# Row maxima of the attention softmax, taken over half of the heads at a time

## What is computed

```python
q = split_heads(x @ wq + bq)                 # h = 8 heads of 48
k = split_heads(x @ wk + bk)
v = split_heads(x @ wv + bv)
scores = jnp.einsum('bhqd,bhkd->bhqk', q, k) * scaling
scores = scores + attn_bias[:, None, :, :]   # attn_bias is the adjacency
attn = jax.nn.softmax(scores, axis=-1)
ctx = jnp.einsum('bhij,bhjd->bhid', attn, v)
...
x = _rmsnorm(x + attn_out, alpha1, gamma1)
ff = jax.nn.silu(x @ w1 + b1) @ w2 + b2
x = _rmsnorm(x + ff, alpha2, gamma2)
```

## Time and profile before

| what | value |
|---|---|
| median of 3 runs | 3242.74 us (3239.6 to 3253.91) |
| the profiled execution, its own time | 3253.83 us |
| span of that execution, first to last instruction | 3252.0 us |
| mean granted TensorE clock in it | 0.969 of full speed |
| TensorE matmul busy, share of the span | 2958.8 us, 91% |
| VectorE busy | 1908.7 us, 59% |
| ScalarE busy | 1540.4 us, 47% |
| GpSimd busy | 1444.2 us, 44% |

### The profile page before, as it was taken

The page is one execution under the profiler, slowest core; times in us unless marked ns, Lnnn a source line. Parts: engine busy times, 40 slices in busy tenths (PEclk is TensorE's granted clock), DMA queues, the critical chain, the costliest instruction groups (busy, mean ns, idle before and its releaser), DMA issues. The chain is left out here.

```text
span 3252.0 us, 63751 instructions
## 1 busy us (share of the span) xinstructions
PE 2958.8 (91%) x21571; PEld 2841.3 (87%) x21571; DVE 1908.7 (59%) x3165; ACT 1540.4 (47%) x3998; POOL 1444.2 (44%) x1406
## 2 busy tenths in 40 slices
PE   3999999999999999999999757788899999999986
PEld 3899999999999999999999747688899999999983
DVE  4456565565656565656555457455676766666754
ACT  3354545455454545454545334355454444454530
POOL 0334344444444343434444447200466766666650
PEclk9999999999999999999999979899999999999998
DMA  4001001010101010100101056455666666666869
GB/s 123 29 23 44 24 31 37 24 44 24 44 24 44 24 44 23 43 24 29 38 24 39 28 230 271 132 169 156 200 210 205 197 190 185 209 192 193 261 225 362
DMA packets 293655, 359.10 MB, mean 110 GB/s; under 512 B 24328, under 2 KB 285960, under 8 KB 293512
## 3 DMA queue, kind: packets, MB, share of 16 engines
q1 hardware_dynamic: 284840, 344.92, 33.0%
q10 hardware_dynamic: 8704, 12.58, 1.0%
HBM read 286.14 MB, written 71.30 MB: 110 GB/s over the span
## 5 line engine op out<-in xcount | busy, mean ns | idle before, releaser
L1611 PE MATMUL u_bank<-x_in,x_w 128*128 128x256 f32 x4608 | 585.4, 286 | 27.9 <-issue 17.4
L1611 PEld LDWEIGHTS u_bank<-x_in,x_w 128*128 128x128 f32 x4608 | 578.8, 195 | 30.3 <-issue 30.3
L929 POOL TENSOR_TENSOR hT_lo<-h_tmp,hT_hi 128x512 fp32r<-128x512 f32 x192 | 247.8, 1291 | 471.0 <-DVE hT_hi L817 471.0
L1764 POOL TENSOR_TENSOR x_w<-raw,x_w 128x768 fp32r<-128x768 f32 x128 | 274.1, 2141 | 296.2 <-DVE x_w L1707 296.2
L1768 POOL TENSOR_TENSOR x_aT<-x_act,x_aT 128x512 fp32r<-128x512 f32 x128 | 299.3, 2338 | 217.2 <-ACT x_aT L1676 217.2
L390 PE MATMUL m_bank<-yT_hi,w_hi 128*128 128x256 f32 x1152 | 339.7, 295 | 0.0
L1667 ACT ACTIVATE x_gelu<-u_bank,x_b1T 128x256 f32<-128x256 f32 x256 | 121.3, 474 | 444.8 <-PE u_bank L1611 444.8
L390 PE MATMUL m_bank<-yT_lo,w_hi 128*128 128x256 f32 x1152 | 324.5, 282 | 0.0
L390 PE MATMUL m_bank<-yT_hi,w_lo 128*128 128x256 f32 x1152 | 323.7, 281 | 0.0
L663 ACT ACTIVATE h_tmp<-m_bank,b1c 128x256 f32<-128x256 f32 x384 | 160.6, 470 | 330.1 <-PE m_bank L390 329.7
L1623 PE MATMUL o_bank<-x_w,x_aT 128*128 128x384 f32 x1536 | 289.6, 336 | 1.8 <-POOL x_aT L1768 1.8
(11 more groups left out here) (213 smaller groups left out, 7343.0 us busy)
## 6 DMA issues: line engine op xcount, KB each, us to landing
raw<-in_L_ffn_w_dram SPq DMA_DIRECT2D x384, 384.0 KB, 5.0
ws_raw<-in_L_ffn_w_slot_dram SPq DMA_DIRECT2D x8, 2304.0 KB, 9.4
x_in<-in_x_dram SPq DMA_DIRECT2D x32, 384.0 KB, 3.5
x_res<-in_x_dram SPq DMA_DIRECT2D x32, 384.0 KB, 4.2
residual<-f_sb SPq DMA_DIRECT2D x32, 384.0 KB, 2.5
yn<-yn_sb SPq DMA_DIRECT2D x32, 384.0 KB, 2.5
yk<-yn SPq DMA_DIRECT2D x16, 768.0 KB, 11.1
se<-se SPq DMA_DIRECT2D x16, 768.0 KB, 3.3
```

The source lines that it names most:

```text
L929: nc.gpsimd.tensor_tensor(hT[i % 3][1][:], h_tmp[i % 2][:], hT[i % 3][0][:].bitcast(F32), ALU.subtract).then_inc(hl.sem, 1)
L1611: mm = pe.matmul(u_bank[n % BANKS][:, g, :], w1s[i % 2][a][:, c, g, c2 * P:(c2 + 1) * P], xT[e % 2][b][:, c, :], start=c == 0 and j == 0, ...
L1764: nc.gpsimd.tensor_tensor(w2s[i % 2][1][:], raw2[i][:], w2s[i % 2][0][:].bitcast(F32), ALU.subtract).then_inc(w2_lo.sem, 1)
```

## The change

Every addition of the adjacency is followed directly by a reduction over the four heads of its half, and there is one signal for each half (four in a step, where there were two). ScalarE waits in front of each group of four exponentials for the maxima of that half. The same elements are reduced, and the values are the same.

```diff
-    sc_ok, mx_ok, p_ok, rs_ok = S("scores", 4), S("row_max", 2), S("exp", 16), S("recip", 2)
+    sc_ok, mx_ok, p_ok, rs_ok = S("scores", 4), S("row_max", 4), S("exp", 16), S("recip", 2)
...
             def exps(g, t):
-                act.wait_ge(mx_ok.sem, mx_ok.at(g, t + 1))
                 for par in range(2):
+                    act.wait_ge(mx_ok.sem, mx_ok.at(g, 2 * t + par + 1))
                     for m in range(H // 2):
...
                                             adj_sb[:, t, :].unsqueeze(1).broadcast_to([P, H // 2, P]), ALU.add).then_inc(sc_ok.sem, 1)
-                dve.wait_ge(sc_ok.sem, sc_ok.at(g, 2 * t + 2))
-                nc.vector.tensor_reduce(nmax[:, t, :], s_sb[t][:].rearrange("p a m n -> p (a m) n"), X_AXIS, ALU.max,
-                                        negate=True).then_inc(mx_ok.sem, 1)
+                    dve.wait_ge(sc_ok.sem, sc_ok.at(g, 2 * t + par + 1))
+                    nc.vector.tensor_reduce(nmax[:, t, par * (H // 2):(par + 1) * (H // 2)], s_sb[t][:, par, :, :], X_AXIS,
+                                            ALU.max, negate=True).then_inc(mx_ok.sem, 1)
```

## The result

| | before | after |
|---|---|---|
| median of the runs made together (4 and 4) | 3244.45 us | 3210.32 us (3205.1 to 3213.1) |
| ratio, after to before | | 0.9889, 95% interval 0.9863 to 0.9916 |
| profiled execution, its own time / span | 3253.83 / 3252.0 us | 3213.1 / 3211.3 us |
| one step of the layer | 55.64 us | 54.52 us |

The change makes the kernel faster by 1.1%, 34 us. The forecast was 36.5 us less and 3206 us, in a range of 3197 to 3230. It started from the 3242.74 of three runs; from the 3244.45 of four the same gain would have given 3208.

The account below looks back on a forecast made before the run. TensorE was taken to bound the kernel, losing time only while transposes wait for the exponentials. Starting these 1.14 us earlier in 32 steps gives 36.5 us: 3242.74 - 36.5 = 3206 us, range 3197 to 3230.

Parts of the forecast that it names:

- What bounds the kernel: Layer's regular steps: TensorE bounds, losing time only where transposes of the exponentials (L449) wait for them, 32.7 of 1600 us.
- The price of a half: VectorE's maxima over 512 elements: r = 0.69 us, on a line between 0.42 for 256 and 1.22 for 1024.
- the rival that a half costs nearly as much as the whole: VectorE's half reduction at r = 1.22: second maxima gate, gain 0.31 us a step, 10 us, 3233; chance 0.05.
- The first exponential: ScalarE, graph 0: second addition and half a reduction leave its path; it starts 1.14 us earlier, TensorE gaining that each step.
- The second wait: ScalarE, between exponentials 4 and 5: second maxima arrive 0.27 us early, no cost; binds from r = 0.92.
- The formula for r above that bound: When second maxima gate the transposes, TensorE gains 2.75 - 2r us a step; a loss once r passes 1.375.
- VectorE's extra work and what is late next: VectorE does 0.26 us more per graph, 17 us in all, covered by idle time; later consumers keep slacks of 0.3 to 0.9.
- The sum: Whole layer: 32 steps x 1.14 = 36.5 us less, first two steps included; 3242.74 becomes 3206.
- Slower by the count of instructions: VectorE: 64 more reductions each pay a fixed 0.153 us, 10 us over, 3253; chance 0.01.
- The stall that moves: Context or logits wait instead: half the gain lost, 3225, chance 0.07; in full, no gain, 3243, 0.06.
- Slower by the gate: Second maxima gate with r at 1.50: 0.25 us a step lost, 8 us, 3251; chance 0.03.
- The attribution of weight loading's wait to the addition L774: TensorE's wait before the transposes: profile names addition L774 as releaser; set aside because graph 1's first addition ended at 1004.94, before 1006.47.

Follow-up runs that it names:

- the quarters: The changed kernel with graph 0's additions and maxima in four quarters of two heads, a wait for each: step 54.17 us, medians 3202.73 and 3197.88 us.
- where a half took 1.28 us: The changed kernel with each half's reduction made twice in a row, the first into an unread tile: 3246.12 us, ratio 1.0005 to the kernel before.
- graph 1's halves: Against the kernel before, only graph 1 has its maxima in halves: step 55.64 us, 3240.02 us, ratio 0.9996.
- the cut for graph 0: Against the kernel before, only graph 0 has its maxima in halves: step 54.51 us, 3209.6 us, ratio 0.9893.
- with both additions first: The changed kernel's halves and waits, but both additions ahead of both reductions as before: step 54.98 us, 3221.2 us, ratio 0.9924.

## Why the prediction was right

**What bounds the kernel.** Right, and shown from both sides: what was taken from the one wait of the earlier trace rows came out of the step, and work added where VectorE waits cost nothing (one reduction more behind the maxima, 55.64 us). One statement was too low: the idle time is not the whole of what TensorE loses there. The prediction had 1.13 us of idle time, took 1.14 away and left 0.2, which does not add up; its gain came from the starts along the chain, and that was the right way. Measured by starts, the waits cost 1.47 us a step before and 0.34 after, and 1.13 is the difference.

**The price of a half.** 0.69 was read off a line through 0.42 and 1.22; it is 0.686, so the rival that a half costs nearly as much as the whole is out. The 256-element reduction of the quarters is 0.42.

**The first exponential.** 1.14 us earlier was forecast and 1.13 measured, the difference a gap of 0.04 instead of 0.02 between addition and reduction. The transposes of the second half should start 4.75 us after the first addition; they start after 4.76. The step fell by 1.12.

**The second wait.** It was to cost nothing, with 0.27 us to spare; it costs nothing, with 987.39 - 987.13 = 0.26 to spare. The formula for r above that bound was borne out where a half took 1.28 us (the first exponential at 2.04 instead of 1.45 after the first addition): 0.17 gained a step, 0.15 by the formula with 1.30 and 0.19 with 1.28.

**VectorE's extra work and what is late next.** No other wait of TensorE appeared. The second addition of graph 1 ends 989.38 + 0.68 - 984.39 = 5.67 us after the first addition of graph 0, against 5.68 forecast. The remaining 0.21 us of wait was forecast as 0.2.

**The sum.** This is the term that was a little off. The step's 1.12 is right, but 32 of them did not arrive: 31 to 33 us lie in the layer (31.2, 33.2 and 30.7 from the first matmul to L560's last, in the three executions after). The first steps gained little; I counted them by their waits and did not look at the clock there, though the first step's transposes took 1.12 us in these rows and the second's 0.66. The median fell by 34.1 against 36.5, within what a median of four runs leaves open (the interval of the ratio is 27 to 44 us).

**The rivals.** Slower by the count of instructions fell with the reduction added to the kernel before, and with graph 1's halves, which are without effect. The stall that moves fell with the wait list. Slower by the gate was shown to be a matter of r: at 1.28 us the gain of a step is down to 0.17. A half of more than 1.375 us, from where the formula has a loss, was not run. The attribution of weight loading's wait to the addition L774, which I had set aside, was rightly set aside: with quarters, the additions of graph 1 start no earlier and the wait is gone.

## What to carry to other kernels

Where the bounding engine waits at the end of a chain through engines that have slack, find the first hand-over at which the next engine could have started on a part, and cut only there: the cut for graph 0 gave all, that for graph 1 nothing, because its consumer came late anyway. A smaller piece brings the first one sooner, and it pays as long as the producer keeps up with the consumer and the bounding engine still waits: a half took VectorE 1.33 us where ScalarE needed 1.55 for its four exponentials, and quarters still gave 0.35 a step more; at quarters the two are level (0.80 against 0.77 us) and the wait is gone. With 1.92 us for a half the producer no longer kept up, and most of the gain was lost. As long as it waits elsewhere, its additional instructions cost nothing. The idle time of the bounding engine understates what a wait costs; the distance between the starts around it does not. Judge an edit of half a per cent by the length of a regular step in the trace, which repeats to 0.01 us, before the medians, which for one kernel came out up to 0.17% apart; but it speaks for the regular steps only, and the first steps and the part behind the layer can hide a few us of it.

## What the runs showed that I had not expected

A reduction that waits for an earlier addition, and not for the one just ahead of it, overlaps with that one: with both additions first it starts 0.60 us after the start of an addition of 0.69, where one that waits for the addition just ahead starts 0.73 after it (985.12 - 984.39). And TensorE's clock in the thin first steps is not the same in each execution: 0.95, 0.70 and 0.50 were granted in the same 10 us of kernels with the same work on TensorE. And a wait costs TensorE more than its idle time, by 0.13 us for the one that is left after the change and by 0.34 for the two before it.
